# Gate and up products of a feed-forward quarter issued alternately, one into either PSUM bank in turn

## What is computed

```
x = x + attention(context, layernorm(x), mask)
n = layernorm(x)
h = silu(n @ w1.T * s1) * (n @ w2.T * s2)     # gate and up, 256 -> 1024
h = gelu(h @ h1.T * s3)                        # 1024 -> 1024
h = gelu(h @ h2.T * s4)                        # 1024 -> 1024
out = x + h @ w3.T * s5                        # 1024 -> 256
```

## Time and profile before

| | us |
|---|---|
| median of 3 runs (907.47 to 908.09) | 908.03 |
| the profiled execution | 908.02 |
| its span from first to last instruction | 906.2 |
| PE busy | 899.8 (99%) |
| DVE busy | 615.1 (68%) |
| ACT busy | 389.8 (43%) |

### The profile page before, as it was taken

One profiled execution on the slowest core, in us unless ns is written; L12 is line 12 of the kernel. 1 busy time (PEld: TensorE's weight loads), 2 busy tenths in 40 slices (PEclk: granted clock), 3 DMA queues, 4 the chain that ended last, 5 costly groups with the idle time before them and its releaser, 6 DMA issues.

```text
span 906.2 us, 20852 instructions
## 1 busy us (share of the span) xinstructions
PE 899.8 (99%) x7600; PEld 864.2 (95%) x7600; DVE 615.1 (68%) x1224; ACT 389.8 (43%) x1100; POOL 76.1 (8%) x101
## 2 busy tenths in 40 slices
PE   9999999999999999999999999999999999999998
PEld 7889999999999999999999999999999999999998
DVE  5887858577585776857667586675857857576453
ACT  5973534435253252623535235253443525455231
POOL 3543000010000100001010010100001000000000
PEclk9999999999999999999999999999999999999999
DMA  9932232412314232142311424113241231303000
GB/s 350 382 115 57 64 85 68 122 53 80 81 46 122 61 97 63 38 122 69 115 41 35 122 69 122 35 58 98 69 122 46 75 85 55 93 24 106 25 13 14
DMA packets 82348, 79.20 MB, mean 87 GB/s; under 512 B 8592, under 2 KB 74896, under 8 KB 82320
## 3 DMA queue, kind: packets, MB, share of 16 engines
q1 hardware_dynamic: 81744, 78.31, 28.0%
q10 hardware_dynamic: 576, 0.52, 0.2%
HBM read 51.55 MB, written 27.26 MB: 87 GB/s over the span
## 4 chain that ended last, share of the span: by engine, by line
PE 94%; ACT 3%; DMA 1%; issue 1%; DVE 1%; SPq 0%; POOL 0%; ACTq 0%; DVEq 0%
PE F L627 56%; PE G L627 7%; PE F L738 7%; PE G L620 6%; PE G L478 5%; PE G L514 5%; PE G L496 2%; PE S L531 2%; PE G L603 2%; ACT pr L886 1%; ACT look_out L945 1%; PE F L514 1%; DMA p_dram<-pb 0%; DMA x_in<-x_t 0%; DMA pr<-p_dram 0%
## 5 line engine op out<-in xcount | busy, mean ns | idle before, releaser
L858 ACT ACTIVATE g<-F,firsts 128x256 f32<-128x256 f32 x250 | 104.5, 471 | 326.8 <-PE F L627 326.6
L627 PE MATMUL F<-hBh,H 128*128 128x256 f32 x1008 | 239.3, 282 | 0.1
L627 PE MATMUL F<-hAh,H 128*128 128x256 f32 x992 | 235.5, 282 | 1.0 <-ACT g L858 1.0
L627 PE MATMUL F<-hBl,H 128*128 128x256 f32 x1008 | 236.3, 279 | 0.0
L627 PE MATMUL F<-hAl,H 128*128 128x256 f32 x992 | 232.6, 279 | 0.0
L627 PEld LDWEIGHTS F<-hBl,H 128*128 128x128 f32 x1008 | 190.0, 189 | 0.4
L627 PEld LDWEIGHTS F<-hBh,H 128*128 128x128 f32 x1008 | 188.9, 187 | 0.6 <-ACT g L858 0.3
L627 PEld LDWEIGHTS F<-hAh,H 128*128 128x128 f32 x992 | 186.0, 187 | 2.2 <-ACT g L858 1.2
L627 PEld LDWEIGHTS F<-hAl,H 128*128 128x128 f32 x992 | 186.9, 188 | 0.3
L1260 DVE CAST hBh<-g 128x512 fp32r<-128x512 f32 x64 | 27.6, 432 | 119.9 <-ACT g L858 119.9
L886 ACT ACTIVATE pr<-pr,nmx 128x128 f32<-128x128 f32 x240 | 92.7, 388 | 1.3 <-DVE nmx L1095 1.1
(11 more groups left out here) (160 smaller groups left out, 1503.2 us busy)
## 6 DMA issues: line engine op xcount, KB each, us to landing
p_dram<-pb SPq DMA_DIRECT2D x30, 512.0 KB, 3.3
pr<-p_dram SPq DMA_DIRECT2D x120, 128.0 KB, 3.2
H_raw<-h SPq DMA_DIRECT2D x16, 512.0 KB, 13.9
cT<-ctx_t SPq DMA_DIRECT2D x14, 512.0 KB, 3.3
x_dram<-xt SPq DMA_DIRECT2D x28, 256.0 KB, 2.3
out<-y SPq DMA_DIRECT2D x32, 128.0 KB, 1.7
x_in<-x_t SPq DMA_DIRECT2D x15, 256.0 KB, 2.7
x2T<-x_dram SPq DMA_DIRECT2D x60, 64.0 KB, 1.9
```

The lines of the kernel that those rows point to most:

```text
L627: return mm(bank, W[0][:, k, cols], part[:, k, :], start=first, stop=last)
L858: fn(g[:, q % 2, m, :], mid_bank(f, q)[:, m, :], ACT.Gelu, scale=scols[:, col:col + 1]).then_inc(gelu_ready, 1)
```

## The change

For every quarter both sets of waits now stand ahead of the first product. Then, for either half, each step of the input and each part of it, one gate product and one up product are issued in turn. gate_done and up_done are raised by the last two products of the quarter. `ffn_group` had no other caller and goes away. The products, their operands, their order within a bank and all other engines' programs stay.

```diff
--- before.py
+++ after.py
@@ -626,16 +626,6 @@
                     return mm(bank, W[1][:, k, cols], part[:, k, :].bitcast(F32), start=first, stop=last)
                 return mm(bank, W[0][:, k, cols], part[:, k, :], start=first, stop=last)
 
-            def ffn_group(bank, W, cols, hi, lo, general, ready=None):
-
-                kk = W[0].shape[1]
-                for k in range(kk):
-                    if ready is not None:
-                        ready(k)
-                    part_product(bank, W, k, cols, hi, k == 0, False, general)
-                    ins = part_product(bank, W, k, cols, lo, False, k == kk - 1, general)
-                return ins
-
             def gate_up(f, q, general):
 
                 gate_bank, up_bank = gate_banks(q)
@@ -646,10 +636,6 @@
                     pe.wait_ge(scaled[0], at("scaled", f - 1, 1))
                 elif q > 1:
                     pe.wait_ge(sil_ready, at("sil_ready", f, 2 * q - 2))
-                for h in range(2):
-                    cols = slice((2 * q + h) * P, (2 * q + h + 1) * P)
-                    ins = ffn_group(gate_bank[:, h, :], (W1, W1_raw), cols, x2h, x2l, general)
-                ins.then_inc(gate_done, 1)
                 if q == 0 and isinstance(f, int) and f == 0:
                     pe.wait_ge(kT_ready, at("kT_ready", 1, 2))
                 elif q == 1 and isinstance(f, int) and f == 0:
@@ -660,8 +646,13 @@
                     pe.wait_ge(g_ready, at("g_ready", f, 2 * q - 2))
                 for h in range(2):
                     cols = slice((2 * q + h) * P, (2 * q + h + 1) * P)
-                    ins = ffn_group(up_bank[:, h, :], (W2, W2_raw), cols, x2h, x2l, general)
-                ins.then_inc(up_done, 1)
+                    for k in range(KD):
+                        for part in (x2h, x2l):
+                            first, last = k == 0 and part is x2h, k == KD - 1 and part is x2l
+                            gate = part_product(gate_bank[:, h, :], (W1, W1_raw), k, cols, part, first, last, general)
+                            up = part_product(up_bank[:, h, :], (W2, W2_raw), k, cols, part, first, last, general)
+                gate.then_inc(gate_done, 1)
+                up.then_inc(up_done, 1)
 
             def middle_bank(f, q):
```

## The result

The changed kernel takes 910.43 us, median of ten runs (910.04 to 911.48), against 908.01 for the kernel before on the same chip (907.2 to 908.1): ratio 1.0029, 95% interval [1.0021, 1.0037], 2.4 us more. The ratios in this text stand as measured beside their intervals; they are not the quotients of the two medians and can differ from them by up to 0.0005. A second measurement gave 910.38 against 907.81, ratio 1.0029 [1.0017, 1.0041]. The profiled execution took 910.36 us, its span is 908.5 us (906.2 before). The prediction was 911.4, in a range of 909.6 to 913.6.

What follows compares the result with a forecast made beforehand. PE was taken as the bound, busy 899.8 of 906.2 us. Ends 1.63, tile 0 0.69, waits and spacing 1.1 gave 3.4 us on 908.03: 911.4 us, range 909.6 to 913.6.

Steps and rivals of the forecast that it cites:

- The ends: Tiles 14 and 15, first middle quarter: PE waits for the SiLU, delayed 0.81 us in each; 1.63 us in all.
- Tile 14 as a whole: Tile 14: the full 0.81 us SiLU delay stays as loss, despite PE's later 0.4 us wait for the probabilities.
- Nothing is taken back: Tile 14: exponentials slip by the same 0.81 us as the SiLU, so the later probabilities wait recovers none of it.
- Tile 0: Tile 0, quarter 3: its SiLU starts later, ACT loses 0.69 us and PE waits that much longer for the first GELU.
- both facts: Tile 0: the moved wait for multiplication 1 holds PE 0.8 us; gate_done on product 15 then delays ACT's SiLU 0.69 us.
- Waits and spacing in tiles 1 to 13: Late key projection (0.05 us a tile, 0.7 for 13) and possibly slower products (1.4 us in 16 tiles): together 1.1 us.
- last sign: Steady tile should take 55.55 to 55.65 us; forecast wrong if it keeps 55.51, falls, or grows by over 0.2.
- only the ends pay: Rival, 11%: tile 0's inspections finish early enough and the key projection is never late; 909.7 to 910.3 us.
- DVE as the bound: Rival, 10%: DVE delays quarter 3 and the key projection, 0.25 us in each of 13 tiles; 913.6 us.
- Shorter spacing: Rival, 7%: alternating banks closes the gate products up from 116.7 to 110 ns; 908.8 us.
- literal reading of the rule: All 64 quarters: by the bank rotation rule alone, 0.81 us would be exposed in each, 52 us; the forecast took less.

Runs made afterwards that it cites:

- gate_held: Kernel before with seven gate, seven up, then each eighth product; old waits, gate_done with product 15, no alternation: 909.4 against 907.8 us, 1.0018.
- bank swap: Changed kernel with quarters 4 and 6 of tiles 14 and 15 changing banks and order: 909.05 against 907.81 us, 1.0014.
- alt_tile0: Kernel before with alternating products in tile 0 alone: 908.66 against 907.68 us, 1.0015.
- alt_loop: Kernel before with alternating products in tiles 1 to 13 alone: 907.73 against 907.68 us, 1.0002.
- alt_tile15: Kernel before with alternating products in tile 15 alone: 908.52 against 907.68 us, 1.0012.
- waits_ahead: Kernel before with both sets of waits ahead of each quarter, products in their old order: 907.96 against 907.8 us, 0.9997.
- after: The changed kernel itself, in its first profile, against the kernel before: 910.43 against 908.01 us, 1.0029.
- up_first: Changed kernel with the up product ahead of the gate product in each pair, gate_done with product 16: 912.42 against 907.8 us, 1.0052.

## Why the prediction was right in sign and range, and a microsecond too high

- **The ends** (1.63 predicted). Right in place, mechanism and size. From gates to middle each end tile grows by 0.85 us (8.48 less 7.63), where 0.81 was taken. `gate_held`, with the late gate_done and the waits at their old place, grows by just 0.81 (8.44). The 0.04 more is quarter 3 held for multiplication 1, as in tile 13: product 15 starts 7.27 us after the first gate product of tile 14, and 7.24 in tile 8 and in `gate_held`. The bank swap brings the 8.48 down to 7.50.
- **Tile 14 as a whole** (0.81 predicted, 0.67 measured in the first pair of traces). "Nothing is taken back" holds for the mechanism: the last write of the probabilities starts 14.89 us after the first gate product before (829.45 less 814.56) and 15.73 after, 0.84 later. The pair of traces hides it, and the reason lies in the kernel before. Its chain in tile 14 ran through the probabilities, with this write (first row) and read (second row):

```profile
829.45 3.96 DMA p_dram<-pb
...
834.72 3.41 DMA pr<-p_dram
```

From the start of the write to the end of that read it took 8.68 us. In the four other kernels that leave tile 14 as it was, alt_tile0, alt_loop, alt_tile15 and waits_ahead, the same way took 7.89 to 8.10 us, PE does not wait for the probabilities at all, and the tile takes 46.08 to 46.09. It is not the write alone: in those four it took 3.48 to 4.02 us. Against those the changed kernel's 47.14 to 47.18 are 1.1 us more. The move to the middle part makes 0.85 of it; the rest is a wait for the probabilities (0.2 in `after`) and the slower spacing of the last section (0.14 us in `after`, 0.28 in its second trace). The 0.4 us of the earlier trace rows was the luck of one execution, and I treated it as a property of the kernel.
- **Tile 0** (0.69 predicted, 0.77 measured, 0.70 in the kernel that changes tile 0 alone). Right, both facts included: the late gate_done alone costs nothing, the moved waits alone about 0.1 us, and moving the mask brings SiLU back by 0.6 of its 0.8 us.
- **Waits and spacing in tiles 1 to 13** (1.1 predicted, 0.08 measured). This is the term that failed, by 1.0 us, and it explains why 911.4 was 1.0 above 910.4. By the prediction's own last sign, that it is wrong if a tile keeps 55.51, this part was wrong. The range held all the same because it was wide enough to take in "only the ends pay" too. The term had two sources. For the key projection I worked out a cover of 0.07, found it exactly in the trace after, and still charged 0.05 a tile since a released engine needs some time. It does, but at this wait the load needs 0.05 us (tile 13 and `up_first`), which fits into 0.07; the 0.28 us to the second product was the wrong figure to hold against it. At quarter 3 the load needs 0.12, out of a cover of 0.18 in tile 8. For the spacing I took a part of the 1.4 ns by which the output products are slower. They too read one moving tile twice running with weights from two tensors, but 16 alternating products take 1.87 us as before, so this order alone does not slow a stream. The output products add into one bank and the gates into two in turn; whether that is the difference is open.
- **The rivals.** "Only the ends pay" named 909.7 to 910.3; with tile 0's cost added, which its range allowed and its words denied, it comes closest to what happened (910.4). DVE as the bound needed multiplication 0 after 484.1 in tile 8's old times; it starts at 484.71 - 0.77 = 483.94. Shorter spacing is refuted by 1.87. Its example was misread, too: the transposes, 110 ns apart, are not the closest products of the trace, since the 32 smaller score products (L531) take 1.17 us together, 29 ns apart; neither says anything of products over 256 columns. The Trainium skill, TensorE: Matmul & The Clock Gate, Back-to-back issue gap, gives N / 2.4 + 2.5 ns for a product alone, by which an estimate for 256 columns is 109 ns, and says that this does not hold in a stream of weight loads and products. Here the stream has 116.7 ns, with one bank and with two in turn.
- **The rule on rotating banks.** The rows say that the evacuation of the gate banks moved by 0.8 us and stayed hidden wherever more work of PE followed. The Trainium skill, Perfetto Trace Analysis, Optimizing Tensor Performance, Matmuls, asks for rotation so that evacuation overlaps the next group. The measurement agrees with it in tiles 14 and 15, where the next products need the bank at once, and in tiles 1 to 12 it shows no cost where the prediction's literal reading of the rule, an estimate of its own, would charge 0.81 us in each quarter.

## What to carry to other kernels

A signal that comes later costs time only where its waiter has nothing else queued: look at the first and the last round of a loop before its body, since here the body of 13 tiles paid 0.08 us and three places paid 2.2. Work the cover out to a hundredth from the timeline, and take off it what the waiter needs behind the release at that very wait: 0.07 us ahead was free where the load needs 0.05, 0.06 ahead was too little where it needs 0.12, and one product later cost 0.1 us a tile. A wait that one execution shows at the end of a chain through memory may be that execution's own; take it from several traces before adding or subtracting it.

## What the runs showed of the hardware that was not expected

The spacing of the same stream of products has two levels, and which one holds can change at a stall. Middle parts of 128 products take 14.94 us (116.7 ns apart) or 15.08 (117.8 ns); in tile 14 the second middle part of three of the fourteen traces is of the slower kind, among them both traces of the changed kernel, and the granted clock is full in all of them. Chain of waits of the changed kernel, tile 14 into tile 15:

```profile
843.85 15.08 PE F L627 x128
...
862.72 1.89 PE G L627 x16
864.60 1.88 PE F L627 x16
```

The gates behind it have 1.89 and 1.88 in place of 1.87. It is no effect of the alternation: the kernel before has it in its last stretch, behind the wait for GELU in tile 15, where the changed kernel has the faster level.

```profile
889.86 3.77 PE F L627 x32
893.63 1.88 PE G L627 x16
```

It is worth 0.14 us for 128 products, enough to blur differences of a few tenths between end tiles. Tile 15 takes 46.19 us in alt_tile15, with some 250 products at the slower level, and 45.94 with the same code in the changed kernel, with some 60; the 190 between them are worth 0.21 us at 1.1 ns each. What picks the level was not tried.
